# An adaptive-norm block with linear attention and a mixture of experts: order of the last routing steps, PE spins, and one bank for the experts' product

## The reference

```
mod = silu(c) @ wmod                       # 4 x (6 x 256): sa, ca, ga, sb, cb, gb
h = layernorm(x) * (1 + ca) + sa           # x: 4 x 2048 x 256
q, k, v = phi(h Wq), phi(h Wk), h Wv       # phi = elu + 1; 16 heads of 16
S += k_t v_t^T ; z += k_t                  # running state over the 2048 positions
out = (S q_t) / max(z q_t, 1e-6)
x = x + ga * (out @ Wo)
h = layernorm(x) * (1 + cb) + sb
top 2 of 8 experts by softmax(h Wr), 1280 places each, in order of position
y = sum over chosen experts of weight * (silu(h Wg) @ Wd[e])
x = x + gb * y
```

## Time and profile before

| | |
|---|---|
| median of 3 runs | 868.64 us (866.63 to 870.15) |
| profiled execution | 870.15 us |
| its span | 868.4 us, mean granted clock 0.977 |
| PE busy | 811.7 us (93%) |
| DVE, ACT, POOL busy | 577.6, 491.2, 480.1 us (67, 57, 55%) |
| attention part, steady | about 42 to 547 us |
| passage | 547 us to the first gate product at 603.5 us |
| experts | 603.5 us to the last matmul, 855.9 us |
| last scatter lands, end | 868.4 us |

### The profile page before, as it was taken

How to read it: one execution, slowest core, us unless ns; L and a number is a source line. 1 busy time by engine, 2 the same in 40 slices (tenths; PEclk the granted TensorE clock), 3 DMA queues, 4 the chain that set the end, 5 groups by cost and what they waited for, 6 DMA issues and landing times.

```text
span 868.4 us, 24557 instructions
## 1 busy us (share of the span) xinstructions
PE 811.7 (93%) x9488; PEld 666.4 (77%) x9488; DVE 577.6 (67%) x1739; ACT 491.2 (57%) x1004; POOL 480.1 (55%) x621
## 2 busy tenths in 40 slices
PE   6899999999999999999999999858999999998994
PEld 4576776777777767767777777647999999998994
DVE  4666677777777867867777767750767756646652
ACT  5556665756756656657657565431655554454551
POOL 2202345664664665656656645554467657657664
PEclk9999999999999999999999999967999999999997
DMA  5578913322332333323222212234376666666653
GB/s 194 173 238 269 308 29 115 87 87 105 81 110 89 84 110 92 83 94 75 66 78 68 54 50 50 58 74 147 74 166 132 148 147 123 147 156 122 137 98 42
DMA packets 71426, 99.02 MB, mean 114 GB/s; under 512 B 7810, under 2 KB 52866, under 8 KB 71320
## 3 DMA queue, kind: packets, MB, share of 16 engines
q1 hardware_dynamic: 38744, 53.93, 23.7%
q0 software_dynamic: 21760, 31.66, 16.1%
q10 hardware_dynamic: 10816, 11.96, 4.4%
HBM read 46.84 MB, written 63.36 MB: 127 GB/s over the span
## 4 chain that ended last, share of the span: by engine, by line
PE 63%; POOL 11%; issue 8%; DMA 6%; DVE 6%; ACT 4%; another core or an unknown queue 1%; POOLq 0%; SPq 0%; ACTq 0%; DVEq 0%
PE PJ L1433 10%; PE MD L1406 7%; PE SCW L1337 6%; PE SCW L1373 6%; PE SCW L1651 5%; PE PJ L1443 5%; POOL out L612 4%; PE SCW L1398 4%; PE SCW L1357 4%; DMA out<-EX,desti 4%; POOL idle L440 3%; PE MD L1347 3%; PE SCW L1666 2%; PE SCW L1363 2%; DVE Sm L964 2%
## 5 line engine op out<-in xcount | busy, mean ns | idle before, releaser
L494 POOL DMA_INDIRECT slot_rows<-Hrow,sloti x128 | 128.4, 1003 | 128.3 <-PE SCW L1363 47.1
L964 DVE TENSOR_TENSOR Sm<-SCW,tri 128x1024 f32<-128x1024 f32 x128 | 150.8, 1220 | 67.7 <-PE SCW L1337 65.9
L612 POOL DMA_INDIRECT out<-EX,desti x80 | 125.5, 1569 | 23.3 <-POOL idle L440 10.5
L1433 PE MATMUL PJ<-hT,w_qkv 128*128 128x512 f32 x384 | 109.9, 419 | 2.4 <-POOL hT L544 2.1
L440 POOL TENSOR_TENSOR idle<-mhalf 128x1 f32<-128x1 f32 x136 | 60.5, 445 | 79.8 <-DVE EX L1267 51.1
L1433 PEld LDWEIGHTS PJ<-hT,w_qkv 128*128 128x128 f32 x384 | 69.8, 190 | 25.0 <-issue 6.7
L1373 PE MATMUL SCW<-Sm,VA 128*17 128x128 f32 x2048 | 81.1, 276 | 0.0
L1406 PE MATMUL MD<-w_og,ATs 128*128 128x256 f32 x256 | 73.4, 409 | 4.8 <-ACT ATs L824 2.9
L678 ACT ACTIVATE EX<-PJ 128x512 f32<-128x512 f32 x64 | 37.9, 593 | 67.3 <-PE PJ L1433 67.3
L1337 PE MATMUL SCW<-QM,KT 32*128 32x256 f32 x1024 | 73.8, 400 | 0.8 <-ACT OTs L839 0.5
L682 ACT ACTIVATE N<-X,nb,rs 128x256 f32<-128x256 f32 x128 | 66.4, 591 | 8.4 <-POOL nb L554 8.1
(11 more groups left out here) (215 smaller groups left out, 1822.9 us busy)
## 6 DMA issues: line engine op xcount, KB each, us to landing
Hrow<-slot_rows SPq DMA_DIRECT2D x32, 516.0 KB
slot_rows<-erow ACTq DMA_DIRECT2D x1, 10400.0 KB, 50.6
...
slot_rows<-Hrow,sloti POOLq DMA_INDIRECT x128
...
```

The costliest lines, as they stand in the source:

```text
L494: pool.indirect_dma_start(xe, bass.IndirectOffsetOnAxis(sloti[:, par, k, t:t + 1], 0), Hrow[:, par, t, :], None, bounds_check=last_slot, o ...
L612: pool.indirect_dma_start(out, bass.IndirectOffsetOnAxis(desti[s % 2][:, a:a + 1], 0), Ys[s % 2][:, a, :], None, bounds_check=TOK - 1, oob ...
L964: dve.tensor_tensor(o.rearrange("p c (k w) -> p c k w", k=2), SCW[:, 2 * pair:2 * pair + 2, :].rearrange("p k (c w) -> p c k w", c=DC), tr ...
L1433: last = mm(PJ[m % 2][:], w_qkv[:, wp, cc, m * P:(m + 1) * P], hT[:, hp, cc, :], start=(cc + i == 0), stop=(cc == DC - 1 and i == len(SPLI ...
```

## The change

It does six things.

1. On DVE the two loops that force routing steps in slots 62 and 63 go; the calls of `between()` that stand among the other operations stay.
2. On PE `positions` of group 14 moves from slot 63 to the head of `last_group`.
3. On POOL the sends of group 13 are in another order: none in slot 62; departure and six sends in slot 63; `last_deviations` of the last group's first three tiles and the last two sends in slot 64. The bound of every send becomes a plain number in place of a register set once.
4. On ACT two of the last group's norms stand ahead of the copy of ATs.
5. In the expert part both halves of the down product go into one bank, with one `y_full` per block. DVE waits for the whole block, POOL waits for both weighted halves and runs one breather per block, not two.
6. PE runs 10 transposes of the identity before its first matmuls and 6 behind them, and 100 in place of 85 before the experts.

```diff
@@ -493,13 +493,28 @@
                 def send_row(t, k, par=1 - gp):
                     pool.indirect_dma_start(
                         xe, bass.IndirectOffsetOnAxis(sloti[:, par, k, t:t + 1], 0), Hrow[:, par, t, :], None,
-                        bounds_check=last_slot, oob_is_err=False).then_inc(sent[par], 16)
+                        bounds_check=SLOTS - 1, oob_is_err=False).then_inc(sent[par], 16)
 
                 paced = tile_ok(n) and group_ok(gn - 3)
                 if paced and q == 0:
                     send_row(0, 0)
                     pool.wait_ge(knt_full, T + 1)
                     send_row(0, 1)
+                if n == TILES - 1:
+                    departure(GROUPS - 3)
+                    send_row(0, 0, 1)
+                    pool.wait_ge(on_full, TILES - 1)
+                    send_row(0, 1, 1)
+                    pool.wait_ge(knt_full, TILES)
+                    send_row(1, 0, 1)
+                    pool.wait_ge(at_full, TILES - 1)
+                    send_row(1, 1, 1)
+                    pool.wait_ge(sent[0], 128 * (GROUPS // 2 - 1))
+                    number(GROUPS - 2)
+                    pool.wait_ge(state_full, TILES)
+                    send_row(2, 0, 1)
+                    pool.wait_ge(op_full, TILES - 1)
+                    send_row(2, 1, 1)
                 def last_deviations(t0, t1, part):
 
                     ts = slice(t0, t1)
@@ -508,22 +523,11 @@
                     pool.wait_ge(pow2, GROUPS - 1 + part)
                     pool.tensor_tensor(nb2[:, ts], nm2[:, ts], rs2[:, ts], ALU.mult).then_inc(rstd2, 1)
 
-                if n == TILES - 1:
-                    pool.wait_ge(sc_full[1], 2 * TILES)
-                    send_row(1, 0, 1)
-                    pool.wait_ge(on_full, TILES - 1)
-                    send_row(1, 1, 1)
-                    pool.wait_ge(knt_full, TILES)
-                    send_row(2, 0, 1)
-                    pool.wait_ge(sent[0], 128 * (GROUPS // 2 - 1))
-                    number(GROUPS - 2)
-                    pool.wait_ge(at_full, TILES - 1)
-                    send_row(2, 1, 1)
-                    pool.wait_ge(state_full, TILES)
+                if n == TILES:
+                    last_deviations(0, GT - 1, 1)
+                    pool.wait_ge(on_full, TILES)
                     send_row(3, 0, 1)
-                    last_deviations(0, GT - 1, 1)
                     send_row(3, 1, 1)
-                if n == TILES:
                     departure(GROUPS - 2)
                     send_row(0, 0, 0)
                     last_deviations(GT - 1, GT, 2)
@@ -562,10 +566,6 @@
                     send_row(3, 0)
                     pool.wait_ge(knt_full, T + 1)
                     send_row(3, 1)
-                if n == TILES - 2:
-                    departure(GROUPS - 3)
-                    send_row(0, 0, 1)
-                    send_row(0, 1, 1)
                 if q == 2 and group_ok(gn - 1) and gn < GROUPS - 1:
                     deviations(rs2, vp2, nm2, nb2, vpe2, pow2, rstd2, G)
                 if q == 2 and group_ok(gn + 2):
@@ -587,7 +587,6 @@
                     modulate()
 
             pool.wait_ge(consts, N_CONST)
-            last_slot = pool.to_reg(SLOTS - 1)
             run_slots(slot_)
 
 
@@ -605,10 +604,10 @@
 
                     pool.wait_ge(y_sent[0], 32 * (ep * BS + (s + 1) // 2))
                     pool.wait_ge(y_sent[1], 32 * (ep * BS + s // 2))
+                pool.wait_ge(breath, 4 * (GROUPS - 2) + S)
+                pool.wait_ge(ys_done, 2 * S + 2)
+                breather(4)
                 for a in range(2):
-                    pool.wait_ge(breath, 4 * (GROUPS - 2) + 2 * S + a)
-                    pool.wait_ge(ys_done, 2 * S + 1 + a)
-                    breather(4)
                     pool.indirect_dma_start(
                         out, bass.IndirectOffsetOnAxis(desti[s % 2][:, a:a + 1], 0), Ys[s % 2][:, a, :], None,
                         bounds_check=TOK - 1, oob_is_err=False, compute_op=ALU.add).then_inc(y_sent[s % 2], 16)
@@ -725,10 +724,11 @@
 
             def last_group():
 
+                for t in (0, 1):
+                    last_norm(t)
                 act.wait_ge(at_full, TILES)
                 act.activation(ATs[:].rearrange("p c i -> p (c i)"), MA[:, 0:D], ACT.Copy).then_inc(at_done, 1)
-                for t in range(GT - 1):
-                    last_norm(t)
+                last_norm(2)
                 act.wait_ge(lgt_full, GROUPS - 1)
                 act.wait_ge(back_full, 2)
                 for cidx in range(DC):
@@ -867,7 +867,7 @@
                     if n >= 2:
 
                         act.wait_ge(hid_lo, 2 * (S - 2) + hh + 1)
-                        act.wait_ge(y_full, 2 * (S - 1))
+                        act.wait_ge(y_full, S - 1)
                     f = slice(2 * hh, 2 * hh + 2)
                     act.activation(hid_raw[s % 2][:, f, :], SC[hh].rearrange("p (f n) -> p f n", f=2),
                                    ACT.Silu).then_inc(silu_done, 1)
@@ -885,7 +885,7 @@
             def down_hi(ep, k, n):
                 act.wait_ge(wd_in[k], 16 * (ep + 1))
                 if n >= 1:
-                    act.wait_ge(y_full, 2 * (ep * 2 + k - 1) * BS)
+                    act.wait_ge(y_full, (ep * 2 + k - 1) * BS)
                 act.activation(WD[k][0], WD_raw[k], ACT.Copy).then_inc(wd_hi, 1)
 
             def step_b(ep, s, n, last):
@@ -1174,8 +1174,6 @@
                         normalise_heads(T, between, lambda: None)
                 elif tile_ok(n - 1):
                     normalise_heads(T, between, between)
-                while TILES - 2 <= n and small[0] < 9:
-                    between()
                 if q == 0 and group_ok(gn + 2) and gn >= 1:
                     ln1_stats(it, G, gp)
                 if stage1 and q >= 2:
@@ -1187,8 +1185,6 @@
                 if tile_ok(n):
                     state(it, T, j)
                 between()
-                while n == TILES - 1 and small[0] < 13:
-                    between()
                 if stage1 and q in (1, 2):
                     phi(G, 2 * (q - 1), npar)
                 between()
@@ -1261,10 +1257,10 @@
 
             def weighted_rows(ep, s):
                 S, par = ep * (2 * BS) + s, s % 2
+                dve.wait_ge(y_full, S + 1)
                 dve.wait_ge(meta, 5 * S + 5)
                 for a in range(2):
-                    dve.wait_ge(y_full, 2 * S + 1 + a)
-                    dve.scalar_tensor_tensor(Ys[par][:, a, :], ((MA, KR), (MD, SB))[par][a][:, 0:D],
+                    dve.scalar_tensor_tensor(Ys[par][:, a, :], (MA, MD)[par][:, a * D:(a + 1) * D],
                                              bs[par][:, 8 + a:9 + a], Xr[s % BS][:, a, D + 4:ROW],
                                              ALU.mult, ALU.mult).then_inc(ys_done, 1)
 
@@ -1297,6 +1293,8 @@
                 for i in range(count):
                     pe.transpose(bank[:, (i % 4) * P:(i % 4 + 1) * P], ident[:], ident[:])
 
+            pe.wait_ge(consts, N_CONST)
+            spin(MD, 10)
             pe.wait_ge(c_silu, 1)
             pe.wait_ge(wm_in[0], 16)
             for m in range(2 * DC):
@@ -1304,8 +1302,8 @@
                     last = mm(MA[:, m * BATCH:(m + 1) * BATCH], wmod_sb[:, k, m * P:(m + 1) * P], cS[:, k, 0:BATCH],
                               start=(k == 0), stop=(k == DC - 1))
             last.then_inc(mod_mm, 1)
+            spin(MD, 6)
             pe.wait_ge(dve_setup, 2)
-            pe.wait_ge(consts, N_CONST)
 
             def modulation(hh):
                 if hh == 0:
@@ -1526,6 +1524,7 @@
 
             def last_group():
 
+                positions(GROUPS - 2, GROUPS)
                 head_rows(TILES)
                 attention_columns(TILES)
                 out_product(TILES, TILES)
@@ -1615,7 +1614,6 @@
                 if n == TILES - 2:
                     logits(GROUPS - 2, gn, False)
                 if n == TILES - 1:
-                    positions(GROUPS - 2, GROUPS)
                     rows_back(GROUPS - 2, 1)
 
             run_slots(slot_, early)
@@ -1625,7 +1623,7 @@
             pe.wait_ge(w_lo, 2)
             pe.wait_ge(sbd_done, TILES)
             pe.wait_ge(rested, GROUPS)
-            spin(SB, 85)
+            spin(SB, 100)
 
             def slot_columns(ep, s, n):
                 S, par = ep * (2 * BS) + s, s % 2
@@ -1663,10 +1661,10 @@
                 for a in range(2):
                     for f in range(FC):
                         for i, (hp, wp) in enumerate(SPLIT):
-                            last = mm(((MA, KR), (MD, SB))[par][a][:, 0:D], hid[par][hp][:, f, a * P:(a + 1) * P],
+                            last = mm((MA, MD)[par][:, a * D:(a + 1) * D], hid[par][hp][:, f, a * P:(a + 1) * P],
                                       WD[k][wp][:, f, :], start=(f + i == 0),
                                       stop=(f == FC - 1 and i == len(SPLIT) - 1))
-                    last.then_inc(y_full, 1)
```

(1 more changed line is left out.)

## The result

| | before | after |
|---|---|---|
| median of the runs | 867.81 us (4 runs, 866.63 to 870.15) | 881.23 us (4 runs, 876.28 to 885.76) |
| ratio to before | | 1.0127, 95% interval 1.0089 to 1.0164 |
| profiled execution (its span) | 870.15 (868.4) | 880.69 (878.8) |

Forecast were 871.5 us and a range of 864 to 877. The change made the kernel slower by 1.3%, and the time lies outside the range. The ratio is not the quotient of the two medians: it takes in 20 runs of after (876.0 to 885.8 us) and leaves out a 21st of 891.7 us that fell in a slower state.

A forecast was written before the change was run, and what follows sets the result against it. TensorE was busy 93%; the prediction looked to its idle places, the attention-to-expert passage and the expert part. Terms 3.9 + 0.3 - 0.5 + 0 - 0.8 + 0 = +2.9 us on the 868.64 median gave 871.5 us, range 864 to 877.

The forecast's parts named there:

- the first part: Opening section on what bounds the kernel; claimed steady attention slots are touched only in one operand of each send.
- part 2: Sends with a plain-number bound: one more sequencer instruction each, eight of group 15 on the path, +0.3 us (0 to 0.4).
- Rival (a): Slots 62 and 63: the unexplained 2.1 us lag before `state` goes in the new order; 868.0 us, chance 0.17.
- Part 1: Routing steps in slots 62 and 63 and `positions`: later mask delays the last tile's heads and division, +3.9 us (0.4 to 5).
- the prediction's own sign: Group 14's mask on DVE: starts at 570 or later if the routing claim holds, wrong if before 568.5.
- Part 3: PE's spins at the opening and ahead of the experts: smaller idle gap keeps the clock up, -0.5 us (-2.0 to +0.5).
- The opening: The 10 and 6 spins around PE's first matmuls: taken as 0, at best a gain of 1.1 us.
- Part 4: Experts' product in one bank: late start and missing breathers nearly cancel, -0.8 us (-4.9 to +7).
- a tail of 0: End of the expert part: the last two sends start about when the last send did before, 0 us.
- the breather: POOL's pause between a block's two sends: without it 1.33 to 1.85 us apart, taken as 1.6, before 1.94.
- Rival (c): Expert part: landings `slot_meta` waits for come 1 us later; 879.3 us at seven boundaries, 875.4 at half, chance 0.17.
- its sign: Experts from the first gate to PE's end: over 256 us would show the prediction wrong; 252.4 before.

The follow-up runs named there:

- e10: Kernel before with the plain-number bound only on the three sends of each slot with n%4 = 2; 879.3 us, ratio 1.0110.
- e9: Kernel before with the bound's register written afresh behind each transfer, so no move stands between wait and transfer; 870.0 us, ratio 1.0006.
- e2: Kernel before with only the bound of the routing sends made a plain number; 864.0 us, ratio 1.0075.
- e3: Kernel after without the 10 + 6 opening spins; 862.2 us, ratio to before 1.0087.
- e5: Kernel after, unchanged, measured again on a chip where before takes 855.9 us; 864.8 us, ratio to before 1.0084.
- e1: Kernel before with only the 10 + 6 opening spins added; 856.6 us, ratio 0.9995.
- e6: Kernel before with an unused register move ahead of each transfer; the trace lacks the move, so it is before again; 855.7 us, ratio 0.9965.
- e7: Kernel before with an unused register move behind each transfer; the trace lacks the move, so it is before again; 855.7 us, ratio 0.9977.
- e8: Kernel before with the experts' edit alone (product in one bank, one signal a block, one breather); 857.0 us, ratio 0.9995.
- e16: Kernel before with only the routing edits: DVE loops, `positions`, order of POOL's and ACT's last steps; 858.5 us, ratio 1.0029.
- e4: Kernel after with the bound of the routing sends in a register again; 854.7 us, ratio to before 0.9984.
- e11: Kernel before with the plain-number bound only on the five sends of slots with n%4 = 0 and 1; 870.2 us, ratio 1.0008.
- e13: Kernel before with the last send of each slot with n%4 = 2 moved between the two deviations; 861.3 us, ratio 1.0057.
- e17: Repeat, on another chip, of before with the last send of slots n%4 = 2 moved between the deviations; 858.2 us, ratio 1.0027.

## Why the prediction was wrong

**The step that failed** is a sentence of the first part: "The steady attention slots hold nothing that the change touches but one operand of each send." It put 120 of the 128 sends at no cost, and part 2 priced only the eight of group 15. The runs put 9.6 us there in the first comparison, 12.4 in e10 (545.4 against the 533.0 of e9), and 4.9 to 7.0 on the fast chip (e2, e3 and e5 against 522.2, the mean of e1, e6, e7 and e8). Three things were missing. First, where a move stands: I took its length, 0.03 us, from the earlier trace rows, but behind a wait it moves the start of the transfer by 0.53, and behind the transfer by nothing (e9). Where sends follow each other without a wait, as in the earlier trace rows, it hides under the one before: they are still 1.28 apart, as predicted. Second, who is behind POOL in a steady slot. Third, what POOL's operations run into when they come later: DVE's operation on the fast chip (1.60 us in place of 1.08), the stop on the slow one. That the steady slots are sensitive to POOL could be read from the trace of before: it has third slots of 8.5 and of 9.25 us side by side, with the sends at other distances. Rival (a) said that no other slot shows the unexplained lag. In its size, 2.1 us from PE's write to `state`, that is so. But the same trace has 0.80 to 0.89 us there in the seven whole third slots, and a stop inside PE's products in the five torn ones, where e1 has 0.10 and none.

**Part 1**, +3.9 us (0.4 to 5). After, with the 9.62 us taken off: mask 567.6 and division 569.6, against 566.21 and 568.49 and the 570.4 and 572.4 forecast.

```profile
574.02 0.29 DVE L989 SCALAR_TENSOR_TENSOR Sbd<-SB,carry,headmask 128x68 f32<-128x68 f32 x1 [3.27 <-remote]
...
577.20 0.19 DVE L1060 TENSOR_TENSOR masks<-oh 128x32 bf16<-128x32 f32 x1
...
579.23 0.42 DVE L980 TENSOR_TENSOR An<-MD,rden 128x256 f32<-128x256 f32 x1
```

The mechanism is there: the mask comes late, and `head_rows` right behind it (577.61). But the lag of slot 62 went and only that of slot 63 stayed, so half of rival (a) came true, and the term measured +1.1 at the division. By the prediction's own sign (wrong if the mask comes before 568.5) the 3.9 was too large. That the new order removed the lag is not shown: e9 has the routing of before and slot 62 without a lag (8.74 us, before 10.25), and against its division after is 1.7 later (36.0 us behind the scores of slot 60, e9 34.3). Where before has no lag in slot 62 either, it is +2.4 up to the first rows (e16 and e4, 66.0, against 63.6 in e8). The plain bound adds 1.4 in this passage (67.4 in e3, 66.0 in e4), for which I had 0.3: in after POOL lets the last group go at 597.76, before at 585.51, +2.6 with the 9.62 taken off, while DVE's last place step is only 1.2 later.

**Part 3**, -0.5. The gap before the first rows is 0.74 us, the granted clock stays at 1.00 in the four microseconds from there (0.50), and the first gates come sooner than the earlier trace rows had them:

```profile
598.10 11.53 PE L1294 MATMUL SB<-ident 128*128 128x128 f32 x78 [4.54 <-POOL idle L456]
610.02 2.61 PE L1294 MATMUL SB<-ident 128*128 128x128 f32 x22 [0.39 <-issue]
613.38 0.66 PE L1635 MATMUL PJ<-ident,Hrow 128*128 128x128 f32 x4 [0.74 <-DMA Hrow<-slot_rows]
615.45 3.11 PE L1649 MATMUL SCW<-KS,w_g 128*128 128x256 f32 x24
618.75 3.09 PE L1649 MATMUL SCW<-VS,w_g 128*128 128x256 f32 x24
```

```profile
613.38:617.38 4.00, 3.25 (x24) 2.77 (x25) 1.38 (x2) 2.54 (x4) 0.00 (x0) 1.00 1.02 386
```

The second gate starts 5.37 us after the first rows, before 7.20: -1.8, the good end of the bounds. It is not a gain to count on: in e5, the same program, the gap was 2.77 us, the clock fell and the gate took 4.20. Of the six profiles with 100 spins three have 3.11 us (gaps of 0.74 to 1.28) and three 4.20 to 4.54 (gaps of 2.44 to 2.77); and e9, with 85 spins and a gap of 1.15, took 4.44, so the gap alone does not decide. The opening brought nothing (12.05, 1.94 us, as the earlier trace rows; e1): 0, as taken. The Trainium skill's rule that the slow clock is the default and activity releases it (TensorE: Matmul & The Clock Gate, "Part 1: The HAM clock gate (the "warmup" mystery)") would, as the prediction read it, have made these transposes fast. They were not, and no run here tests the rule on them: the granted clock is 1.00 from 12 to 16 us both before and after. Why they take 1.94 us stays open.

**Part 4**, -0.8 and a tail of 0. Sends of a block are 1.87 us apart (702.33, 704.20), before 1.94, so the breather was worth 0.07 and not 0.3. The one wait of PE for DVE at the down product (line, who waited for whom, us in total, times, longest):

```profile
PE SCW L1664 <- DVE QS L1235: 2.6, 1, 2.6
```

That is 2.6 us in total in place of the 4.9 of the earlier trace rows. Over all profiles the column "experts" has a mean of 251.4 us in the seven with the edit (247.3 to 255.7) and 254.4 in the thirteen without (251.4 to 257.8): -3.0, with a scatter as large as the difference. The tail was wrong: both last halves wait for PE's last product, and the two sends follow 1.86 us apart.

```profile
865.11 0.88 DVE L1263 SCALAR_TENSOR_TENSOR EX<-MD,VA,QT 128x256 f32<-128x256 f32 x2 [0.55 <-PE MD L1664]
865.83 1.55 POOL L611 DMA_INDIRECT out<-EX,desti  x1 [0.31 <-issue]
866.84 0.77 POOL L440 TENSOR_TENSOR idle<-mhalf 128x1 f32<-128x1 f32 x1
867.76 1.55 POOL L611 DMA_INDIRECT out<-EX,desti  x1 [0.16 <-issue]
869.62 1.55 POOL L611 DMA_INDIRECT out<-EX,desti  x1 [0.30 <-issue]
```

In both kernels POOL still had a scatter of the block before to start, at 865.83 here and 855.38 before. That is 0.76 us behind PE's last product (865.07), where it was 0.52 ahead of it (855.90). The late start of each block's first scatter, 1.3 us, which I had myself, is passed on to the end: +1.2, as e8 shows too (4.6 against 3.4). Rival (c) did not come: from the first gate to PE's end it is 249.6 us (615.45 to 865.07), before 252.4, and its sign was 256.

The parts that I had priced came to +0.7 us of span in the first comparison (2.76 - 3.21 + 1.18), against +2.9, with part 1 taken too large and the tail too small. So the forecast was carried past its range by the one part that had no term.

**What stays open**: what stops PE, ACT and DVE together on some chips. Shown is that the plain bound on the three sends of the third slots makes all twelve torn and costs the time (e10, e11). Argued is that the stop belongs to the last send: it lies at the same time behind it in torn and whole slots. The distance of 1.28 us sorts which slots are torn, but it was not changed on such a chip, and e13 and e17, made for it, ran where nothing is torn. The first gap of 0.2 us in the torn slots of after and e10 has no explanation either.
